# Two attention layers over sixteen batches: weighted sums taken for two groups of heads in one visit, and the transposed maxima moved to the bank of the scores

## The chip, the cores and the metric

The kernel runs on one core of a Trainium2 chip. The metric is the device time of one launch in microseconds (us), the median of several executions. Besides it there is one profiled execution, from which every row below is taken.

## What is computed

Two cross-attention layers follow each other for each of 16 batches. Queries come from `x` (112 rows of 320), keys and values from a context of 375 rows of 192. Cut to what matters:

```python
def _mha(q, k, v, heads):                      # layer 0: 8 heads of 40; layer 1: 20 heads of 16
    scores = jnp.einsum('bhqd,bhkd->bhqk', qh, kh) * d ** -0.5
    probs = jax.nn.softmax(scores, axis=-1)
    return jnp.einsum('bhqk,bhkd->bhqd', probs, vh)
# layer 0
enc, ca = ctx[:, :371], ctx[:, 371:]           # 371 keys, and 4 token rows
hs  = _mha(x @ Wq, enc @ Wk, enc @ Wv)
ca1 = _mha(Q, x, x)        # Q from (ca, Wq_ca): an attention over the 112 rows of x
ca2 = _mha(ca1 @ Wq, ca @ Wk_ca, ca @ Wv_ca)
x1  = (hs + ca2) @ Wout + b_out + x
# layer 1
out = _mha(x1 @ Wq1, ctx @ Wk1, ctx @ Wv1) @ Wo + bo + x1
```

## The kernel before

All engines' programs are written out by hand, in one common order. An iteration t handles parts of several batches, so that independent work stands side by side. It has seven **slots** (0 to 6), and each slot scores one **group** of four heads: in slots 0 and 1 the two groups of layer 0 of batch t, in slots 2 to 6 the five groups of layer 1 of batch t-1. `NUMBER` counts the groups in that order.

A group goes through four steps. `scores` (two heads at a time, "pair 0" and "pair 1", into the two banks of `bankS`) lets VectorE take the negated row maxima (`maximum`, line 773, one reduction per pair). One slot later `transpose_m` (L1172) turns the 112x4 maxima into 4x112, VectorE copies them to `mT` (`copy_mT`, L779), and a DMA of ScalarE's queue (`place_m`) puts them as a row into the queries. Two slots after scoring (`LAG`, the `late` group), `shifted_scores` makes the transposed scores with the maximum subtracted in `bankST` (L1187 layer 0, L1193 layer 1), ScalarE takes the exponentials (`exps`, L573, L574, L577) into one of two halves of `PT` (in `arena`), and `attend` (L1225) makes the weighted sums in `bankO`, whose copy to SBUF is `copy_o` (L790). `attend` issues 12 `matmul` calls per group (24 instructions on the chip, as the operands are fp32), each on only 64 (layer 0) or 32 (layer 1) columns of the array; calls on different columns run at the same time. One `attend` with what surrounds it is called a visit here.

Between these steps, in four **phases** of each slot, stand the **units**: projections and the rest, which take turns in two PSUM banks `bankX0` and `bankX1`. A unit can begin only when the unit two places ahead of it in the list has been drained from its bank (`bank_drained`). The units that matter here, by slot (phases 2 and 3 come after pair 1 of the scores, and `attend` stands between phases 2 and 3):

```python
    ([("V1_0", -1)], [("q1T_0", -1)], [("V1_1", -1)], [("W2", 1), ("PV2", 0)]),                  # slot 0
    ...
    ([("K1_1", 0)], [("S3", 0), ("S2_0", 1)], [("N1b", -2)], [("S2_1", 1)]),                     # slot 2
    ([("K1_2", 0)], [("K0_0", 1)], [("hn1T", -2)], [("K0_1", 1)]),                               # slot 3
    ([("K0_2", 1)], [("p3T", 0), ("N0", 0)], [("out1", -2)], [("q0T_0", 1)]),                    # slot 4
    ([("hn0T", 0), ("V0_0", 1)], [("q0T_1", 1)], [("out0", 0)], [("T2_0", 1)]),                  # slot 5
    ([("x1T", 0), ("V0_1", 1)], [("T2_1", 1)], [("q1", 0)], [("V0_2", 1)]),                      # slot 6
```

S2_0 and S2_1 (L1111) are the scores of the attention over `x`: VectorE takes their maxima (L837), and ScalarE drains each with four exponentials (L595, each with a short read of its sum). K0, K1, V0, V1, q0, q1, out0 and out1 are projections (all L1005). q0T_0, q0T_1 (L1071) and the q1T units (L1078) are transposes of queries; ScalarE drains q0T (L658), and ScalarE and VectorE drain q1T (L666, L829). ScalarE and VectorE drain q1 (L653, L765). N0, N1a and N1b (L1095) transpose the finished sums, hn0T, hn1T and x1T (L1087) the normalised ones. W2 is L1105.

`transpose_m` writes the first 112 columns of `bankO`, which layer 0's weighted sums use as well, so before the change it waits until the last visit's sums are copied (`o_copied`), and `attend` waits until the transposed maxima are copied (`mT_copied`).

Of the kernel before, what the change touches and what calls it, by code (L numbers as in the profile page):

```python
# [85 lines left out]
NUMBER = {g: n for n, g in enumerate(GROUPS)}  # L86

# [24 lines left out]
def xattn_kernel(nc, xT, xpad, ctxT, caS, caT, w_all, w_ca, wqT, bd96, consts, bias, out):  # L112
    g_rows = nc.dram_tensor("g_rows", [B, 3, 32, HID], F32, kind="Internal").ap()

    with ExitStack() as ctx:
# [101 lines left out]
        bank_mT = bankO[0:GROUP, 0:SQ]  # L217
# [334 lines left out]
        def _(act):  # L552
# [10 lines left out]
            def exps(g):  # L563
# [35 lines left out]
            def unit(name, b):  # L599
# [27 lines left out]
                elif kind == "V0":  # L627
                    if i == 0 and b == 0:
                        act.wait_ge(zeroed, 3)
                    elif i == 0:  # L630
                        act.wait_ge(pv_done, NUMBER[0, b - 1, 1] + 1)
# [3 lines left out]
                elif kind == "V1":  # L635
                    if i == 0 and b < 2:
                        act.wait_ge(zeroed, 6 + b)
                    elif i == 0:
                        act.wait_ge(pv_done, NUMBER[1, b - 2, G1 - 1] + 1)
# [91 lines left out]
        def _(dve):  # L731
# [49 lines left out]
            def copy_o(g):  # L781
                layer, b, k = g
                n = NUMBER[g]
                dve.wait_ge(pv_done, n + 1)
                if layer == 0:
                    dst, src = o0T[:, 2 * k:2 * k + 2, :].rearrange("p c q -> p (c q)"), bankO[:, 0:2 * SQ]
                else:
                    at = (2 + n % 2) * SQ
                    dst, src = o1T[:, k, :], bankO[:, at:at + SQ]
# [120 lines left out]
            for t in ITERATIONS:  # L910
                for i in range(SLOTS):
                    g, before, late = scored_at(t, i), scored_at(t, i, 1), scored_at(t, i, LAG)
# [16 lines left out]
                    if late:  # L929
                        copy_o(late)  # L930
# [15 lines left out]
        def _(pe):  # L946
# [61 lines left out]
            def unit(name, b):  # L1008
# [80 lines left out]
                elif kind in ("N0", "N1a", "N1b"):  # L1089
                    layer, k = {"N0": (0, 1), "N1a": (1, 3), "N1b": (1, 4)}[kind]  # L1090
                    pe.wait_ge(o_copied, NUMBER[layer, b, k] + 1)
# [45 lines left out]
            def scores(g, pair):  # L1137
# [25 lines left out]
            def transpose_m(g, attended):  # L1163
                n = NUMBER[g]
                pe.wait_ge(max_done, 2 * n + 2)
                if n > 0:
                    pe.wait_ge(mT_copied, n)
                else:
                    pe.wait_ge(g_split, 4)
                if attended > 0:  # L1170
                    pe.wait_ge(o_copied, attended)
# [27 lines left out]
            def attend(g, transposed):  # L1199
                layer, b, k = g  # L1200
                n = NUMBER[g]
                pe.wait_ge(exp_done, n + 1)
                pe.wait_ge(mT_copied, transposed)
                if n > 0:
                    pe.wait_ge(o_copied, n)
                if k == 0:
                    for i in range(NKC):
                        pe.wait_ge(bank_drained[bank(f"V{layer}_{i}", b)], drained(f"V{layer}_{i}", b))
                src = PT[:, n % 2]
                if layer == 0:  # L1210
                    at_once = [(c, j) for pair in range(2) for c in range(NKC) for j in (2 * pair, 2 * pair + 1)]
                else:
                    at_once = [(c, j) for c in range(NKC) for j in range(GROUP)]
                for c, j in at_once:
                    h = GROUP * k + j
                    if layer == 0:
                        keys = KC if c < 2 else KC - NTOK
                        dst = bankO[64 * (j % 2):64 * (j % 2) + 64, (j // 2) * SQ:(j // 2 + 1) * SQ]
                        v = v0[0:keys, c, 64 * h:64 * h + 64]
                    else:  # L1220
                        keys = KC
                        at = (2 + n % 2) * SQ
                        dst = bankO[32 * j:32 * j + 32, at:at + SQ]
                        v = v1[b % 2][0:keys, c, 32 * h:32 * h + 32]
                    last = nc.tensor.matmul(dst, v, src[0:keys, c, SQ * j:SQ * j + SQ], start=(c == 0),  # L1225
# [118 lines left out]
```

## Time and profile before

| | |
|---|---|
| time, 3 runs | 755.02, 755.55, 756.1 us; median 755.55 |
| profiled execution | 753.38 us, span of its core 751.5 us |
| TensorE matmul / weight load busy | 703.0 us (94%) / 610.3 us (81%) |
| VectorE / ScalarE / GpSimd busy | 472.3 / 404.0 / 295.5 us |
| mean granted TensorE clock | 0.983 of full speed |

The span reaches from the first to the last instruction of the core. PE is TensorE's matmul, PEld its weight load, which normally runs ahead of the matmul before it ends; a busy PE is no proof of a PE at its peak. A row of the timeline gives the start in us from the start of the span, the duration, engine, line, operation, output and inputs, shapes and count, and in brackets the idle time of the engine just ahead of it with what ended it. Idle time matters only on the chain that sets the end.

### The profile page before, as it was taken

The numbers are of one execution on the slowest core, as the hardware profiler recorded it, in microseconds if no ns is written. First come the engines' busy times: TensorE is split into PE (matmuls) and PEld (weight loads), VectorE is DVE, ScalarE is ACT, GpSimd is POOL, SyncE is SP. The second block draws the span as 40 slices with busy tenths as digits, with TensorE's granted clock in tenths as the row PEclk, the third lists the DMA queues.
The fourth block names the chain that finished last, engine by engine and source line by source line (L and its number), as shares of the span: only waits on it lengthen the run. The fifth ranks groups of instructions, "written<-read, shape, count | busy, mean of one in ns | idle before, by whom it ended". The sixth has DMA issues, their size and how long they took to land.

```text
span 751.5 us, 18194 instructions
## 1 busy us (share of the span) xinstructions
PE 703.0 (94%) x6924; PEld 610.3 (81%) x6924; DVE 472.3 (63%) x1028; ACT 404.0 (54%) x923; POOL 295.5 (39%) x401
## 2 busy tenths in 40 slices
PE   8787999999999999999999999999999999999975
PEld 5586888888888888888888888888888888888763
DVE  2653666657576665757576575756667575766662
ACT  2454555555565555565555555556555555654432
POOL 5485662444334253433325344323524542330300
PEclk9889999999999999999999999999999999999996
DMA  9533553443516244252524434261533425051400
GB/s 325 175 96 96 112 133 75 107 80 79 133 47 143 62 119 95 67 118 54 137 60 125 92 80 103 62 142 45 136 81 94 89 76 129 20 137 28 87 7 11
DMA packets 52387, 72.45 MB, mean 96 GB/s; under 512 B 12128, under 2 KB 44256, under 8 KB 52304
## 3 DMA queue, kind: packets, MB, share of 16 engines
q1 hardware_dynamic: 44832, 60.34, 31.7%
q0 software_dynamic: 6144, 9.25, 6.5%
q10 hardware_dynamic: 1328, 1.71, 0.6%
q8 instruction: 57, 0.93, 0.5%
q14 instruction: 26, 0.21, 0.1%
HBM read 20.60 MB, written 4.26 MB: 33 GB/s over the span
## 4 chain that ended last, share of the span: by engine, by line
PE 69%; ACT 13%; DVE 8%; issue 3%; POOL 1%; DMA 1%; SPq 1%; ACTq 0%; POOLq 0%
PE bankX L1005 28%; PE bankO L1225 8%; PE bankST L1193 7%; ACT arena L577 7%; PE bankS L1159 6%; PE bankST L1187 5%; ACT arena L595 3%; DVE negmax L773 2%; DVE q1T L829 2%; PE bankX L1118 2%; PE bankX L1125 2%; PE bankX L1087 2%; PE bankS L1156 2%; ACT q1T L666 2%; PE bankX L1071 2%
## 5 line engine op out<-in xcount | busy, mean ns | idle before, releaser
L773 DVE TENSOR_REDUCE negmax<-bankS 112x2 f32<-112x750 f32 (+1 forms) x224 | 208.7, 932 | 57.0 <-PE bankS L1159 32.7
L494 POOL DMA_DIRECT2D k_stack<-stage x192 | 96.6, 511 | 181.5 <-DVE stage L809 153.9
L577 ACT ACTIVATE arena<-bankST 125x1344 f32<-125x1344 f32 x80 | 103.5, 1294 | 30.9 <-PE bankST L1193 30.9
L1225 PE MATMUL bankO<-arena,v 125*32 125x112 f32 (+2 forms) x2688 | 107.2, 264 | 6.2 <-ACT arena L577 4.4
L1225 PEld LDWEIGHTS bankO<-arena,v 125*32 125x32 f32 (+2 forms) x2688 | 81.2, 117 | 29.0 <-issue 12.7
L1159 PE MATMUL bankS<-k_stack,q1T 112*112 112x376 f32 x320 | 87.8, 355 | 4.1 <-DVE negmax L773 3.0
L1005 PE MATMUL bankX<-ctx_hi,WH 128*120 128x376 f32 (+2 forms) x192 | 69.0, 360 | 3.0 <-DVE qn L765 2.2
L457 POOL TENSOR_TENSOR w2bd<-w2s,cst 96x896 fp32r<-96x896 f32 x16 | 29.9, 1870 | 98.4 <-DVE w2s L765 98.4
L1005 PE MATMUL bankX<-WH,ctx_hi 128*125 128x320 f32 x192 | 66.1, 344 | 0.1
L1193 PE MATMUL bankST<-q1T,k_stack 112*125 112x224 f32 x480 | 65.4, 272 | 0.0
L1005 PE MATMUL bankX<-ctx_hi,WL 128*120 128x376 f32 (+2 forms) x192 | 64.0, 334 | 0.0
L1193 PEld LDWEIGHTS bankST<-q1T,k_stack 112*125 112x125 f32 x480 | 62.0, 188 | 0.8 <-DMA q1T<-mT 0.4
L1005 PE MATMUL bankX<-WL,ctx_hi 128*125 128x320 f32 x192 | 58.5, 312 | 0.0
L1159 PEld LDWEIGHTS bankS<-k_stack,q1T 112*112 112x112 f32 x320 | 49.4, 177 | 8.8 <-DVE negmax L773 6.5
L829 DVE TENSOR_SCALAR q1T<-bankX,odd_rows 128x448 fp32r<-128x448 f32 (+1 forms) x48 | 29.1, 606 | 41.7 <-ACT q1T L666 41.2
L595 ACT ACTIVATE arena<-bankX,negmax 112x112 f32<-112x112 f32 x128 | 43.6, 354 | 21.7 <-DVE negmax L837 21.6
L1005 PE MATMUL bankX<-WH,act_hi 128*112 128x320 f32 x144 | 46.7, 325 | 3.3 <-DVE act_hi L866 1.4
L483 POOL TENSOR_TENSOR xb<-xp,bias_sb 112x320 f32<-112x320 f32 x16 | 13.9, 867 | 88.7 <-DVE x L860 88.6
L779 DVE CAST mT<-bankO 4x112 fp32r<-4x112 f32 x112 | 29.0, 259 | 30.0 <-PE bankO L1172 30.0
L1187 PEld LDWEIGHTS bankST<-q0T,k_stack 121*125 121x125 f32 (+1 forms) x384 | 46.0, 187 | 0.0
L619 ACT ACTIVATE stage<-bankX 128x376 fp32r<-128x376 f32 (+1 forms) x48 | 23.1, 482 | 41.7 <-PE bankX L1005 41.0
L1187 PE MATMUL bankST<-q0T,k_stack 121*125 121x112 f32 (+1 forms) x384 | 44.9, 266 | 0.0
(141 smaller groups left out, 1545.8 us busy)
## 6 DMA issues: line engine op xcount, KB each, us to landing
k_stack<-stage SPq DMA_DIRECT2D x96, 176.2 KB
k_stack<-stage SPq DMA_DIRECT2D x192, 70.5 KB, 2.6
k_stack<-stage POOLq DMA_DIRECT2D x192, 47.0 KB, 2.0
ctx_raw<-in_ctxT SPq DMA_DIRECT2D x16, 376.0 KB, 3.3
k_stack<-stage SPq DMA_DIRECT2D x48, 117.5 KB
xp<-in_xpad SPq DMA_DIRECT2D x16, 224.0 KB, 3.3
x_raw<-in_xT SPq DMA_DIRECT2D x16, 168.0 KB, 2.4
out<-x1b SPq DMA_DIRECT2D x16, 140.0 KB, 3.2
```

What stands on the lines that cost most here:

```text
L457: nc.gpsimd.tensor_tensor(w2bd[:, :, :], w2s[:, :].bitcast(F32).unsqueeze(1).broadcast_to((96, H0, SQ)), mask96.unsqueeze(2).broadcast_to( ...
L494: pool.dma_start(dst, src).then_inc(k1_stacked_pool[b % 2], 16)
L577: nc.scalar.activation(dst[0:KC], bankST[0:KC, :, 0:GROUP * SQ], ACT.Exp).then_inc(exp_done, 1)
L595: last = nc.scalar.activation(prob2[0:SQ, h, :], X[0:SQ, (h % 4) * SQ:(h % 4 + 1) * SQ], ACT.Exp, bias=negmax2[:, h:h + 1], accum_out=sum2 ...
L773: nc.vector.tensor_reduce(negmax[:, n % 2, 2 * pair:2 * pair + 2], bankS[0:SQ, :, 0:keys], axis=AX, op=ALU.max, negate=True).then_inc(max_ ...
L779: nc.vector.tensor_copy(mT[:, n % MT_BUFS, :], bank_mT).then_inc(mT_copied, 1)
L829: nc.vector.tensor_scalar(q1T[:, 4 * i:4 * i + g, 1, :], X[:, 0:g * SQ].rearrange("p (h q) -> p h q", h=g), odd_rows[:, :], None, ALU.mult ...
L1005: last = nc.tensor.matmul(dst, lhs, rhs, start=(n == 0), stop=(n == len(passes) - 1))
L1159: last = nc.tensor.matmul(bankS[0:SQ, j, 0:SKP], q1T[0:ROWS1, h // 2, h % 2, :], k1_stack[b % 2][0:ROWS1, h // 2, :], start=True, stop=True)
L1187: last = nc.tensor.matmul(bankST[0:keys, c, SQ * j:SQ * j + SQ], k0_stack[0:M_ROW0 + 1, h, KC * c:KC * c + keys], q0T[0:M_ROW0 + 1, h, :], ...
L1193: last = nc.tensor.matmul(bankST[0:KC, c, 2 * SQ * pair:2 * SQ * pair + 2 * SQ], k1_stack[b % 2][0:ROWS1, 2 * k + pair, KC * c:KC * c + KC ...
L1225: last = nc.tensor.matmul(dst, v, src[0:keys, c, SQ * j:SQ * j + SQ], start=(c == 0), stop=(c == NKC - 1))
```

## The change

`EPISODES` groups the groups: the two of layer 0 together, and of layer 1 the first two, the next two and the last alone. `attended_at` gives an episode only at the slot in which its last group is late. So `attend` and `copy_o` run four times per batch, in slots 3, 5, 0 and 1, in place of seven times. `shifted_scores` and `exps` keep their places. The sums of two groups stand side by side in `bankO` and are copied by one instruction.

The transposed maxima go to columns 384 to 495 of the second bank of `bankS`, behind the scores of the pair's second head. `transpose_m` now waits for the maxima of pair 0 of the group being scored (they are read from that bank), no longer for `o_copied`. The second matmul of each `scores` call waits for `mT_copied`.

```diff
+EPISODES = [e for b in range(B + 1) for e in
+            ([[(0, b, 0), (0, b, 1)]] if b < B else []) +
+            ([[(1, b - 1, 0), (1, b - 1, 1)], [(1, b - 1, 2), (1, b - 1, 3)], [(1, b - 1, 4)]] if b > 0 else [])]
+EPISODE = {g: n for n, e in enumerate(EPISODES) for g in e}
+def attended_at(t, i):
+    late = scored_at(t, i, LAG)
+    return EPISODES[EPISODE[late]] if late and EPISODES[EPISODE[late]][-1] == late else None
...
-        bank_mT = bankO[0:GROUP, 0:SQ]
+        bank_mT = bankS[0:GROUP, 1, SKP + 8:SKP + 8 + SQ]
...
-                    act.wait_ge(pv_done, n - 1)
+                    act.wait_ge(pv_done, EPISODE[GROUPS[n - 2]] + 1)
...
-                    if late:
-                        copy_o(late)
+                    if attended_at(t, i):
+                        copy_o(attended_at(t, i))
...
                 for j in range(2):
                     h = GROUP * k + 2 * pair + j
+                    if j == 1 and transposed > 0:
+                        pe.wait_ge(mT_copied, transposed)
...
-            def transpose_m(g, attended):
+            def transpose_m(g, scoring):
                 n = NUMBER[g]
-                pe.wait_ge(max_done, 2 * n + 2)
+                if scoring:
+                    pe.wait_ge(max_done, 2 * NUMBER[scoring] + 1)
+                else:
+                    pe.wait_ge(max_done, 2 * n + 2)
...
-                if attended > 0:
-                    pe.wait_ge(o_copied, attended)
...
-                    if late:
-                        attend(late, transposed)
-                        attended = NUMBER[late] + 1
+                    if attended_at(t, i):
+                        attend(attended_at(t, i))
```

Lines move by 12 to 16: L1225 is L1241 after the change, L1111 is L1123, L1159 is L1173, L1005 is L1017, L1095 is L1107, L1087 is L1099, L1156 is L1170.

First place, TensorE in the second half of slot 2 of a middle iteration, before the change: S2_0, pair 1 of the scores, N1b, the visit, S2_1, and pair 0 of slot 3.

```order
L1111 MATMUL bankX<-w2bd,ca_st 112x448 [waits w2_expanded,ca_split,bank_drained1]
L1159 MATMUL bankS<-k_stack,q1T 112x376 [waits max_done]
L1159 MATMUL bankS<-k_stack,q1T 112x376
L1095 MATMUL bankX<-cst,o1T 112x128 [waits o_copied,bank_drained0]
L1225 MATMUL bankO<-arena,v 64x112 [waits bank_drained1,bank_drained0,o_copied,mT_copied,exp_done]
L1225 MATMUL bankO<-arena,v 64x112 x11
L1111 MATMUL bankX<-w2bd,ca_st 112x448 [waits bank_drained1]
```

The same place after the change:

```order
L1123 MATMUL bankX<-w2bd,ca_st 112x448 [waits w2_expanded,ca_split,bank_drained1]
L1173 MATMUL bankS<-k_stack,q1T 112x376 [waits max_done]
L1173 MATMUL bankS<-k_stack,q1T 112x376 [waits mT_copied]
L1107 MATMUL bankX<-cst,o1T 112x128 [waits o_copied,bank_drained0]
L1123 MATMUL bankX<-w2bd,ca_st 112x448 [waits bank_drained1]
```

The visit of twelve calls between S2_0 and S2_1 is gone; S2_1 still waits until its bank (`bank_drained1`, that of S2_0) is drained.

Second place, TensorE in slot 3 right behind, before the change: hn1T, the visit for the second group of layer 0, then K0_1.

```order
L1087 MATMUL bankX<-cst,hn 128x112 [waits bank_drained1,bank_drained0]
L1087 MATMUL bankX<-cst,hn 128x112
L1087 MATMUL bankX<-cst,hn 64x112
L1225 MATMUL bankO<-arena,v 64x112 [waits o_copied,mT_copied,exp_done]
L1225 MATMUL bankO<-arena,v 64x112 x11
L1005 MATMUL bankX<-ctx_hi,WH 120x376 [waits bank_drained1]
```

The same place after the change:

```order
L1099 MATMUL bankX<-cst,hn 64x112
L1241 MATMUL bankO<-arena,v 64x112 [waits bank_drained0,bank_drained1,exp_done,o_copied]
L1241 MATMUL bankO<-arena,v 64x112 x11
L1241 MATMUL bankO<-arena,v 64x112 [waits exp_done]
L1241 MATMUL bankO<-arena,v 64x112 x11
L1017 MATMUL bankX<-ctx_hi,WH 120x376 [waits bank_drained1]
```

Here the twelve calls of the first group now stand ahead of those of the second.

Third place, TensorE from the end of q1 in slot 6 to V1_0 in slot 0, before the change:

```order
L1005 MATMUL bankX<-WL,act_hi 112x320
L1225 MATMUL bankO<-arena,v_1 32x112 [waits o_copied,mT_copied,exp_done]
L1225 MATMUL bankO<-arena,v_1 32x112 x11
L1005 MATMUL bankX<-WH,ctx_hi 125x320 [waits bank_drained0]
L1005 MATMUL bankX<-WH,ctx_lo 125x320
L1005 MATMUL bankX<-WL,ctx_hi 125x320
L1005 MATMUL bankX<-WH,ctx_hi 125x320
L1005 MATMUL bankX<-WL,ctx_hi 125x320
L1156 MATMUL bankS<-k_stack,q0T 112x372 [waits bank_drained0,k0_stacked,max_done]
L1156 MATMUL bankS<-k_stack,q0T 112x372
L1005 MATMUL bankX<-WH,ctx_hi 125x320 [waits bank_drained1]
```

The same place after the change:

```order
L1017 MATMUL bankX<-WL,act_hi 112x320
L1017 MATMUL bankX<-WH,ctx_hi 125x320 [waits bank_drained0]
L1017 MATMUL bankX<-WH,ctx_lo 125x320
L1017 MATMUL bankX<-WL,ctx_hi 125x320
L1017 MATMUL bankX<-WH,ctx_hi 125x320
L1017 MATMUL bankX<-WL,ctx_hi 125x320
L1170 MATMUL bankS<-k_stack,q0T 112x372 [waits bank_drained0,k0_stacked,max_done]
L1170 MATMUL bankS<-k_stack,q0T 112x372 [waits mT_copied]
L1017 MATMUL bankX<-WH,ctx_hi 125x320 [waits bank_drained1]
```

V0_2 now follows q1 directly, and V1_0 (the last row) waits for the bank of q1 with one visit less ahead of it.

## Rows read from the trace of the kernel before

**Rows 1.** The page, part 1: busy time, share, instructions of each engine.

```profile
PE 703.0 (94%) x6924; PEld 610.3 (81%) x6924; DVE 472.3 (63%) x1028; ACT 404.0 (54%) x923; POOL 295.5 (39%) x401
```

**Rows 2.** Waits, all engines: us in total, times, longest.

```profile
PEld bankO L1225 <- issue: 12.7, 63, 0.2
...
PE bankX L1095 <- DVE stage L814: 7.4, 15, 0.5
...
PEld bankX L1111 <- ACT arena L595: 7.0, 13, 0.5
```

**Rows 3.** Timeline, second half of slot 2 of the iteration from 299 us.

```profile
301.86 0.44 PE L1111 MATMUL bankX<-w2bd,ca_st 96*112 96x448 f32 x1
...
302.40 0.61 DVE L837 TENSOR_REDUCE negmax<-bankX 112x4 f32<-112x448 f32 x1
...
302.54 0.13 PEld L1095 LDWEIGHTS bankX<-cst,o1T 128*112 128x112 f32 x1 [0.22 <-DVE p L846]
...
302.82 1.19 PEld L1225 LDWEIGHTS bankO<-arena,v 125*64 125x64 f32 x24 [0.15 <-issue]
...
303.05 0.35 ACT L595 ACTIVATE arena<-bankX,negmax 112x112 f32<-112x112 f32 x1 [0.30 <-DVE negmax L837]
...
304.29 0.21 ACT L595 ACTIVATION_READ_ACCUMULATOR arena<-bankX,negmax 112x1 f32 x1
304.55 0.17 PEld L1111 LDWEIGHTS bankX<-w2bd,ca_st 96*112 96x112 f32 x1 [0.54 <-ACT arena L595]
```

**Rows 4.** Timeline, S2_0 one iteration later.

```profile
345.17 0.44 PE L1111 MATMUL bankX<-w2bd,ca_st 96*112 96x448 f32 x1
```

**Rows 5.** Timeline, the visit in slot 3 and what follows.

```profile
308.98 1.16 PEld L1225 LDWEIGHTS bankO<-arena,v 125*64 125x64 f32 x24 [0.17 <-ACT arena L574]
...
310.29 0.18 PEld L1005 LDWEIGHTS bankX<-ctx_hi,WH 128*120 128x120 f32 x1
```

**Rows 6.** Timeline, end of slot 4 and beginning of slot 5.

```profile
316.17 0.31 PE L1005 MATMUL bankX<-WL,act_hi 128*112 128x320 f32 x1
316.40 0.54 PEld L1225 LDWEIGHTS bankO<-arena,v 125*32 125x32 f32 x24 [0.20 <-issue]
...
317.12 0.60 PE L1071 MATMUL bankX<-cst,qn 112*120 112x112 f32 x4
...
317.75 0.55 ACT L658 ACTIVATE q0T<-bankX 120x448 fp32r<-120x448 f32 x1 [2.76 <-PE bankX L1071]
...
318.35 0.18 PEld L1005 LDWEIGHTS bankX<-WH,ctx_hi 128*125 128x125 f32 x1 [0.24 <-ACT q0T L658]
```

**Rows 7.** Timeline, end of slot 6 to V1_0 in slot 0.

```profile
327.68 0.70 ACT L653 ACTIVATE qn<-bankX 112x640 fp32r<-112x640 f32 x1 [0.27 <-PE bankX L1005]
...
328.42 0.49 DVE L765 SCALAR_TENSOR_TENSOR qn<-bankX,qn 112x320 fp32r<-112x320 f32 x1 [0.97 <-ACT qn L653]
...
329.30 0.18 PEld L1005 LDWEIGHTS bankX<-WH,ctx_hi 128*125 128x125 f32 x1
```

**Rows 8.** Timeline, slot 0: drain of q1T_0, and W2 behind the visit.

```profile
332.80 0.68 DVE L829 TENSOR_SCALAR q1T<-bankX,odd_rows 128x448 fp32r<-128x448 f32 x1 [1.39 <-ACT q1T L666]
...
333.54 0.63 PEld L1105 LDWEIGHTS bankX<-x_raw,bd 128*96 128x96 f32 x6 [0.49 <-DVE q1T L829]
```

**Rows 9.** Timeline, slot 5: copy of the maxima and pair 1.

```profile
320.14 0.26 DVE L779 CAST mT<-bankO 4x112 fp32r<-4x112 f32 x1 [0.52 <-PE bankO L1172]
...
320.25 0.58 PE L1159 MATMUL bankS<-k_stack,q1T 112*112 112x376 f32 x2
...
320.67 0.31 PE L1005 MATMUL bankX<-WH,act_hi 128*112 128x320 f32 x1
```

**Rows 10.** Timeline, slot 4: maximum of pair 0, transpose, N0.

```profile
312.52 0.93 DVE L773 TENSOR_REDUCE negmax<-bankS 112x2 f32<-112x750 f32 x1
...
313.10 0.26 PE L1172 MATMUL bankO<-cst,negmax 112*4 112x112 f32 x1
...
313.96 0.40 PEld L1095 LDWEIGHTS bankX<-cst,o0T 128*112 128x112 f32 x4 [0.73 <-DVE stage L814]
```

More of the change, by code:

```diff
@@ L911, in _ @@
                 for i in range(SLOTS):
-                    g, before, late = scored_at(t, i), scored_at(t, i, 1), scored_at(t, i, LAG)
+                    g, before = scored_at(t, i), scored_at(t, i, 1)
                     if g:
@@ L1090, in unit @@
                     layer, k = {"N0": (0, 1), "N1a": (1, 3), "N1b": (1, 4)}[kind]
-                    pe.wait_ge(o_copied, NUMBER[layer, b, k] + 1)
+                    pe.wait_ge(o_copied, EPISODE[layer, b, k] + 1)
                     cols = [o0T[:, c, :] for c in range(4)] if layer == 0 else [
@@ L1135, in unit, with scores @@
                 last.then_inc(unit_filled, 1)
-            def scores(g, pair):
+            def scores(g, pair, transposed):
                 layer, b, k = g
@@ L1197, in shifted_scores, with attend @@
                 last.then_inc(st_done, 1)
[L1199 to L1203, printed above, removed]
+            def attend(groups):
+                n = EPISODE[groups[0]]
                 if n > 0:
                     pe.wait_ge(o_copied, n)
[L1206 to L1211, printed above, removed]
-                else:
-                    at_once = [(c, j) for c in range(NKC) for j in range(GROUP)]
-                for c, j in at_once:
-                    h = GROUP * k + j
+                else:
+                    pe.wait_ge(g_split, 4)
+                for g in groups:
+                    layer, b, k = g
+                    pe.wait_ge(exp_done, NUMBER[g] + 1)
+                    if k == 0:
+                        for i in range(NKC):
+                            pe.wait_ge(bank_drained[bank(f"V{layer}_{i}", b)], drained(f"V{layer}_{i}", b))
+                    src = PT[:, NUMBER[g] % 2]
@@ L1225, in attend @@
-                    last = nc.tensor.matmul(dst, v, src[0:keys, c, SQ * j:SQ * j + SQ], start=(c == 0),
-                                            stop=(c == NKC - 1))
+                        at_once = [(c, j) for pair in range(2) for c in range(NKC) for j in (2 * pair, 2 * pair + 1)]
+                    else:
+                        at_once = [(c, j) for c in range(NKC) for j in range(GROUP)]
+                    for c, j in at_once:
+                        h = GROUP * k + j
+                        if layer == 0:
+                            keys = KC if c < 2 else KC - NTOK
+                            at = (2 * k + j // 2) * SQ
+                            dst = bankO[64 * (j % 2):64 * (j % 2) + 64, at:at + SQ]
+                            v = v0[0:keys, c, 64 * h:64 * h + 64]
+                        else:
+                            keys = KC
+                            at = (2 + k % 2) * SQ
+                            dst = bankO[32 * j:32 * j + 32, at:at + SQ]
+                            v = v1[b % 2][0:keys, c, 32 * h:32 * h + 32]
+                        last = nc.tensor.matmul(dst, v, src[0:keys, c, SQ * j:SQ * j + SQ], start=(c == 0),
+                                                stop=(c == NKC - 1))
@@ L1249, in _ @@
                     if g:
-                        scores(g, 0)
+                        scores(g, 0, transposed)
                     for u in units_of(t, i, 0):
@@ L1255, in _ @@
                     if before:
-                        transpose_m(before, attended)
+                        transpose_m(before, g)
                         transposed = NUMBER[before] + 1
@@ L1260, in _ @@
                     if g:
-                        scores(g, 1)
+                        scores(g, 1, transposed)
                     for u in units_of(t, i, 2):
                         unit(*u)
-                    if late:
-                        attend(late, transposed)
-                        attended = NUMBER[late] + 1
+                    if attended_at(t, i):
+                        attend(attended_at(t, i))
                     for u in units_of(t, i, 3):
```

28 lines of the change are left out of this document (9 added, 19 removed).

## Prediction

> **What bounds the kernel now.** I read the page's busy times first. TensorE's matmuls are busy for 94% of the span, VectorE 63%, ScalarE 54% [rows 1]. So TensorE's queue sets the end, except where it stands still. The list of waits then says where: in 15 iterations N0 waits 0.5 us each for the drain of K0_2, and 13 times the weight load of S2_1 stands 0.54 us for ScalarE's exponentials. A third entry is of another kind: 63 times the weight loads stop 0.2 us ahead of a visit for nothing that the profile shows [rows 2]. Last I read the timeline of one middle iteration. From one S2_0 to the next it is 43.31 us [rows 3, 4]; this period, paid about 15 times, is what the change has to move. The question at each of the three visits that vanish is: is the next thing on TensorE free to start at once, or does it wait for an engine that doesn't get faster?
>
> **What a visit costs.** In slot 4 the last matmul of out1 starts at 316.17. Matmuls of this kind follow each other at about 0.15 us, so the next unit could start at 316.32; behind the visit it starts at 317.12 [rows 6]. A visit of layer 1 thus costs 0.80 us, of which 0.54 us are its 24 weight loads. A second group in the same visit costs that 0.54 only, if all 48 run at the same pitch. The rest, 0.26 us, is entering and leaving. In layer 0 the 24 loads take 1.16 to 1.19 us, with 0.15 us of stop ahead and 0.15 us behind (308.98 + 1.16 = 310.14, next load 310.29) [rows 3, 5].
>
> The Trainium skill (TensorEngine Tiling (Array Packing), Key Properties) says that changing the tiling mode drains TensorE. The stops of 0.15 to 0.20 us ahead of each visit agree with it. By that rule alone three visits fewer are a plain gain; what it would give stands below as a rival, worked out from rows.
>
> **Slots 2 and 3 (layer 0).** The visit in slot 2 goes, and its 24 instructions come back in slot 3. In slot 2 the visit stands between N1b and S2_1. S2_1 needs S2_0's bank. S2_0 starts at 301.86, VectorE takes its maxima from 302.40 to 303.01, ScalarE's four exponentials run from 303.05 to 304.50, and S2_1's load starts at 304.55 [rows 3]. Nothing in this chain waits for the visit. So S2_1 starts at 304.55 whether the visit is there or not: the visit, 1.19 us of loads and the stop ahead of it, was free, and its removal gives 0. Instead TensorE's load stream stands from 302.67 (end of N1b's load) to 304.55, 1.88 us in place of 0.54. In slot 3 the same 24 instructions cover nothing: what follows, K0_1, starts at 310.29, 0.15 us after the last load [rows 5], so all 1.16 us show. The wait of N0 in slot 4 doesn't absorb them, since its chain (K0_1 and K0_2 on TensorE, their drains on ScalarE and VectorE) begins after the visit. Term A: **+1.16 us**. Bounds: +0.8 if the visit's own stops vanish as well (two of 0.15), +1.4 if the second group costs what a whole visit does.
>
> **Slots 4 and 5.** Behind out1, q0T_0 can start at 316.32 in place of 317.12. ScalarE drains it (its start, 317.75, is set by q0T_0's end, and it had been idle 2.76 us), and that drain sets V0_0 at 318.35 [rows 6]. All of it moves by 0.80. The pair in slot 5 costs 0.54 more. Term B: **-0.26 us**. Bounds: -0.38 (both stops saved: 0.20 ahead and 0.18 between the visit's last load, 316.94, and 317.12) and 0.
>
> **Slots 6 and 0.** Behind q1, V0_2 and pair 0 move up by 0.80. But V1_0 needs the bank of q1: ScalarE copies it from 327.68 to 328.38, VectorE from 328.42 to 328.91 [rows 7], and neither waits for the visit. V1_0 started at 329.30 and can't start before 328.95. So about 0.35 to 0.45 us is gained (its second load comes sooner after a stop), not 0.80; I take 0.40. In slot 0 the pair costs 0.54 more, but W2 behind it stands 0.49 us now, until VectorE has drained q1T_0 at 333.48 [rows 8]. Of that 0.17 us would stay as the stop behind the visit; 0.32 us is absorbed. The pair costs 0.22. Term C: **-0.18 us**. Bounds: -0.37 and +0.14 (nothing absorbed).
>
> **The maxima behind the scores.** New: the second matmul of pair 1 waits for the copy of the maxima. In slot 5 that copy ends at 320.40, the first matmul of the pair starts at 320.25, and the pair's second would start 0.17 us before out0's first at 320.67, so at 320.50, its load some 0.15 us ahead [rows 9]. With about 0.05 us from one engine to the other (as 304.50 to 304.55 above) the load starts 0.05 us late or so. Slots 6 and 0 look the same; in slot 3 it is on the edge; in slots 2 and 4 the copy is early; in slot 1 it is 0.1 us later, but there K1_0 stands for VectorE anyway. Term D: **+0.15 us**. Bounds: 0, and 7 slots x 0.15 = +1.0. Queued behind the waiting matmul is all of TensorE, which is why it counts at all; VectorE's next maximum is late by the same amount.
>
> New as well: `transpose_m` waits for pair 0's maximum. In slot 4 that maximum ends at 313.45 and the transpose started at 313.10, so it is 0.4 us late. Behind it wait p3T and N0, and N0 stands until 313.96 anyway [rows 10]. In the other slots the maximum ends before the transpose starts. Cost 0; without N0's wait it would be 0.4 us. The waits that go (`o_copied` ahead of the transpose, `mT_copied` ahead of the visit) end no stop in the list of waits, so they give nothing. VectorE's three copies fewer are off the path.
>
> **Sum.** 1.16 - 0.26 - 0.18 + 0.15 = +0.87 us per iteration. The stop of S2_1 is there in 13 iterations; the first and last ones have other neighbours, and I count 14 in all: +12.2 us. The profiled execution took 753.38 us (span 751.5, 1.9 around it): 765.6. The median of the runs is 755.55, 2.2 us or 0.3% above the profiled one, so I forecast **767.8, say 768 us**. Bounds added up: lowest 0.8 - 0.37 - 0.37 + 0 = +0.06 per iteration, 757; highest 1.4 + 0 + 0.14 + 1.0 = +2.5, 791. All at one end together is unlikely.
>
> **Rivals.**
> - *The fewer visits pay in full.* Each merged visit saves its two stops, 0.37 us, and nothing becomes late: 3 x 0.37 x 15 = 16.7 us, so 739 us. It decides if S2_1 can start earlier once the visit is gone, that is if ScalarE's exponentials in 303.05 to 304.50 come earlier. Against it: they follow VectorE's maximum, which follows S2_0 and two short operations, not the visit [rows 3]. For it: the other two places do gain. The skill's rule on the drain, named above, would have this outcome. A half form (S2_1's exponentials come 1 us earlier, since some other order results) gives about 753. Together 0.09.
> - *The wait for the copied maxima is the main cost.* The copy stands behind other work of VectorE (drains of K units in slots 2 to 4) and a late one stops TensorE in the middle of pair 1. If each of seven slots loses 0.15 us or more and a restart is paid each time, D is +1.0 or more and the time is 780 or more. It decides where the copy ends over 0.15 us after pair 1 begins; in slot 5 it ends exactly 0.15 after [rows 9]. 0.10.
> - *Covers cancel.* The 1.16 us in slot 3 pushes back work whose inputs then no longer wait (N0's 0.5 us [rows 2], the stops of slot 1), and with B and C the sum is 0: 755.5. Against it: N0's chain begins behind the visit. 0.03.
> - The forecast, slot 2 gives nothing and slot 3 pays: 0.78.
>
> **How the numbers follow.** A change of 0.2%, 1.5 us, is about what a measurement of this kernel can tell. Slower: 0.78 + 0.10, and 0.01 of the half form: 0.89. Within 0.2%: 0.03. Faster: 0.08. The likeliest case alone spans 761 to 776 (terms A and D near their bounds, 0.4 to 1.4 us per iteration times 14 to 15). Below it lies some 0.12, above it 0.10; I reach a little into both: 759 to 778.
>
> **What the changed profile would show.** If right: the period near 44.2 us; at S2_1 (L1123) an idle of about 1.9 us of PEld, released by ScalarE's exponentials, 13 times, some 24 us in the list of waits; one visit of 48 instructions in 2.3 us in slot 3; V1_0 now waits for VectorE's drain of q1; W2 waits for nothing; second scores matmuls wait for L779's copy by under 0.1 us. It is wrong if S2_1 starts less than 2.6 us after S2_0, if the 48 instructions take clearly more or less than twice 1.16 us, if the wait for the copy is long in many slots, or if the granted clock of the middle stretch is lower than now.

## The result, and the profile after

The changed kernel takes 796.82 us (median of 4, 794.62 to 799.32) where the kernel before takes 755.83: ratio 1.0536, 95% interval 1.0502 to 1.057. I had forecast 768 us, 759 to 778. The direction was right and the size was not: 12 us were expected and 41 came.

The page of the changed kernel, span, busy times and the row of granted clock (40 slices, tenths of full speed):

```profile
span 796.8 us, 18066 instructions
...
PE 732.1 (92%) x6924; PEld 639.4 (80%) x6924; DVE 466.4 (59%) x980; ACT 405.5 (51%) x923; POOL 295.1 (37%) x401
...
PEclk9779899999999999798999999798999999799987
```

TensorE runs as many instructions as before [rows 1], yet is busy 29 us longer: the same matmuls take longer in some stretches. The clock row says where. Three stretches make that a sum: the head, up to S2_0 of the third iteration; the middle, twelve iterations; and the tail, the rest. The changed kernel (each row: the stretch and its length in us, busy time and count of PE, PEld, DVE, ACT and POOL, granted clock, share of DMA, GB/s):

```profile
0.00:137.70 137.70, 119.97 (x877) 99.77 (x878) 67.03 (x129) 63.33 (x150) 73.32 (x85) 0.89 0.48 138
137.70:684.80 547.10, 518.77 (x5127) 460.82 (x5126) 337.62 (x720) 296.79 (x685) 205.49 (x288) 0.97 0.37 88
684.80:796.80 112.00, 93.37 (x925) 78.82 (x924) 61.80 (x131) 45.41 (x90) 16.32 (x28) 0.89 0.22 47
```

The same three of the kernel before:

```profile
0.00:128.60 128.60, 112.38 (x877) 92.99 (x878) 67.98 (x133) 63.18 (x150) 73.39 (x85) 0.95 0.52 148
128.60:648.40 519.80, 503.61 (x5126) 444.84 (x5126) 342.13 (x756) 295.79 (x685) 205.79 (x288) 1.00 0.39 93
648.40:751.50 103.10, 87.01 (x925) 72.46 (x924) 62.15 (x139) 45.05 (x90) 16.36 (x28) 0.95 0.24 51
```

So the profiled execution lost 9.1 us in the head, 27.3 in the middle and 8.9 in the tail. Single iterations of the changed kernel, from S2_0 to S2_0:

```profile
271.93:316.16 44.23, 41.86 (x429) 37.12 (x429) 28.09 (x60) 24.64 (x58) 17.10 (x24) 1.00 0.39 92
316.16:364.57 48.41, 46.05 (x429) 41.07 (x429) 28.17 (x60) 24.91 (x58) 17.12 (x24) 0.89 0.36 84
364.57:411.96 47.39, 45.03 (x429) 40.09 (x429) 28.18 (x60) 24.79 (x58) 17.12 (x24) 0.93 0.36 85
```

At full clock an iteration takes 44.23 us against 43.3 before [rows 3, 4]; that is the sum of the prediction, which said 44.2. But in some iterations the clock is granted at 0.89 or 0.93, and they take 3 to 4 us more. Of the twelve of the middle, seven take 44.2 to 44.3 us, one 45.7, two 47.4 and two 48.4. Twelve times 0.92 us are 11 of the 27 us of the middle; the other 16 are the clock.

Now the places of the prediction, in the undisturbed iteration. Slot 2, S2_0 to S2_1, which answers to [rows 3]:

```profile
271.93 0.44 PE L1123 MATMUL bankX<-w2bd,ca_st 96*112 96x448 f32 x1
...
272.60 0.13 PEld L1107 LDWEIGHTS bankX<-cst,o1T 128*112 128x112 f32 x1 [0.21 <-DVE p L858]
...
274.35 0.21 ACT L608 ACTIVATION_READ_ACCUMULATOR arena<-bankX,negmax 112x1 f32 x1
...
274.62 0.17 PEld L1123 LDWEIGHTS bankX<-w2bd,ca_st 96*112 96x112 f32 x1 [1.89 <-ACT arena L608]
274.62 0.46 PE L1123 MATMUL bankX<-w2bd,ca_st 96*112 96x448 f32 x1 [1.70 <-ACT arena L608]
```

S2_1 starts 2.69 us after S2_0, as before the change (301.86 to 304.55 [rows 3]): the visit was free and its removal gave nothing. Slots 3 to 0, which answer to [rows 5 to 8]:

```profile
279.05 2.32 PEld L1241 LDWEIGHTS bankO<-arena,v 125*64 125x64 f32 x48 [0.17 <-issue]
...
281.51 0.18 PEld L1017 LDWEIGHTS bankX<-ctx_hi,WH 128*120 128x120 f32 x1
...
292.52 1.12 PEld L1241 LDWEIGHTS bankO<-arena,v 125*32 125x32 f32 x48 [0.20 <-issue]
...
299.50 0.49 DVE L778 SCALAR_TENSOR_TENSOR qn<-bankX,qn 112x320 fp32r<-112x320 f32 x1 [0.97 <-ACT qn L666]
...
300.05 0.18 PEld L1017 LDWEIGHTS bankX<-WH,ctx_hi 128*125 128x125 f32 x1 [0.53 <-DVE qn L778]
...
303.24 1.12 PEld L1241 LDWEIGHTS bankO<-arena,v 125*32 125x32 f32 x48 [0.19 <-issue]
...
304.52 0.63 PEld L1117 LDWEIGHTS bankX<-x_raw,bd 128*96 128x96 f32 x6 [0.17 <-issue]
```

The 48 loads take exactly twice the 1.16 us of 24, and 1.12 against twice 0.54 in layer 1; there is one stop ahead and one behind. V1_0 now waits 0.53 us for VectorE's drain of q1, and W2 no longer waits for an engine. All of this was forecast.

What wasn't: the same place one iteration later, where the matmuls behind the stop take 0.52 us in place of 0.33.

```profile
318.85 0.71 PE L1123 MATMUL bankX<-w2bd,ca_st 96*112 96x448 f32 x1 [1.69 <-ACT arena L608]
...
319.99 0.52 PE L1017 MATMUL bankX<-ctx_hi,WH 128*128 128x376 f32 x1
...
320.30 0.52 PE L1017 MATMUL bankX<-ctx_lo,WH 128*128 128x376 f32 x1
```

```profile
275.43 0.33 PE L1017 MATMUL bankX<-ctx_lo,WH 128*128 128x376 f32 x1
```

They start 0.31 us apart (319.99 to 320.30) where they start 0.17 apart at full clock: TensorE has gone from 2.4 to 1.2 GHz. Stretches around the stop of S2_1 in the changed kernel:

```profile
300.00:316.85 16.85, 16.77 (x188) 14.93 (x188) 10.11 (x22) 8.77 (x16) 5.10 (x4) 1.00 0.36 85
...
316.85:318.85 2.00, 0.31 (x2) 0.12 (x1) 1.62 (x4) 1.65 (x10) 0.00 (x0) 0.72 0.00 1
318.85:329.00 10.15, 10.15 (x63) 9.63 (x65) 4.72 (x11) 4.41 (x15) 4.79 (x10) 0.55 0.21 38
```

TensorE had been busy without a gap to speak of for 16.85 us at full clock, its matmuls then stood for 1.69 us, and it worked without any gap for 10 us at nearly half speed. A mean of 0.72 over the 2.00 us of the stretch with the stop, between 1.00 and 0.50, means 1.1 us at the lower level: the clock fell inside the stop. It needn't: one iteration on, the stop is as long, but the matmuls behind it still run at full pace, and only the twelve of the shifted scores take 2.41 us in place of 1.40. There the fall came about 1.7 us after TensorE had gone back to work.

```profile
367.26 0.46 PE L1123 MATMUL bankX<-w2bd,ca_st 96*112 96x448 f32 x1 [1.69 <-ACT arena L608]
...
368.59 0.33 PE L1017 MATMUL bankX<-ctx_hi,WL 128*128 128x376 f32 x1
368.76 2.41 PE L1200 MATMUL bankST<-q0T,k_stack 121*125 121x112 f32 x12
```

The stop of S2_1 is there 13 times, 12 times at the start of a period of the middle and once more at 684.8. The clock falls in or just behind six of them.

### The profile page after: what moved, and what is told of

The parts are those of the page before. It is cut to its first block, busy times and chain, and to the rows that moved or that the text cites. A ratio compares the mean times of both kernels' runs of the same rounds, so it can differ in the third digit from the quotient of the medians.

```text
span 796.8 us, 18066 instructions
## 1 busy us (share of the span) xinstructions
PE 732.1 (92%) x6924; PEld 639.4 (80%) x6924; DVE 466.4 (59%) x980; ACT 405.5 (51%) x923; POOL 295.1 (37%) x401
## 4 chain that ended last, share of the span: by engine, by line
PE 78%; ACT 7%; DVE 5%; issue 2%; POOL 1%; DMA 1%; SPq 1%; ACTq 0%; POOLq 0%
PE bankX L1017 30%; PE bankO L1241 12%; PE bankS L1173 7%; PE bankST L1206 6%; PE bankST L1200 6%; ACT arena L590 3%; ACT arena L608 3%; PE bankS L1170 3%; PE bankX L1090 2%; PE bankX L1099 2%; PE bankX L1130 2%; PE bankX L1137 2%; PE bankX L1145 1%; PE bankX L1083 1%; ACT qn L666 1%
## 5 line engine op out<-in xcount | busy, mean ns | idle before, releaser
L1241 PE MATMUL bankO<-arena,v 125*32 125x112 f32 (+2 forms) x2688 | 103.4, 270 | 2.8 <-ACT arena L590 2.8
L1241 PEld LDWEIGHTS bankO<-arena,v 125*32 125x32 f32 (+2 forms) x2688 | 87.9, 123 | 17.1 <-issue 16.7
L1173 PE MATMUL bankS<-k_stack,q1T 112*112 112x376 f32 x320 | 95.7, 378 | 6.0 <-DVE negmax L786 3.9
L1017 PE MATMUL bankX<-ctx_hi,WH 128*120 128x376 f32 (+2 forms) x192 | 73.8, 385 | 2.4 <-ACT arena L608 1.7
L1017 PE MATMUL bankX<-WH,ctx_hi 128*125 128x320 f32 x192 | 66.2, 345 | 3.0 <-DVE qn L778 2.9
L1017 PE MATMUL bankX<-ctx_hi,WL 128*120 128x376 f32 (+2 forms) x192 | 68.8, 358 | 0.0
L1173 PEld LDWEIGHTS bankS<-k_stack,q1T 112*112 112x112 f32 x320 | 55.3, 187 | 13.6 <-DVE negmax L786 6.5
L1017 PE MATMUL bankX<-WL,ctx_hi 128*125 128x320 f32 x192 | 58.1, 310 | 0.0
L638 ACT ACTIVATE stage<-bankX 120x376 fp32r<-120x376 f32 (+1 forms) x48 | 23.2, 484 | 65.7 <-PE bankX L1017 64.8
L792 DVE CAST mT<-bankS 4x112 fp32r<-4x112 f32 x112 | 29.1, 260 | 46.1 <-PE bankS L1185 46.0
L1200 PEld LDWEIGHTS bankST<-q0T,k_stack 121*125 121x125 f32 (+1 forms) x384 | 54.7, 218 | 0.0
L1200 PE MATMUL bankST<-q0T,k_stack 121*125 121x112 f32 (+1 forms) x384 | 53.0, 295 | 0.0
L826 DVE TENSOR_TENSOR stage<-bankX,stage 120x376 fp32r<-120x376 f32 (+1 forms) x48 | 26.2, 545 | 42.1 <-ACT stage L638 42.1
L1017 PE MATMUL bankX<-WH,act_hi 128*112 128x320 f32 x144 | 46.7, 325 | 3.0 <-DVE act_hi L878 1.4
```

What stands on the lines that cost most here:

```text
L792: nc.vector.tensor_copy(mT[:, n % MT_BUFS, :], bank_mT).then_inc(mT_copied, 1)
L1017: last = nc.tensor.matmul(dst, lhs, rhs, start=(n == 0), stop=(n == len(passes) - 1))
L1173: last = nc.tensor.matmul(bankS[0:SQ, j, 0:SKP], q1T[0:ROWS1, h // 2, h % 2, :], k1_stack[b % 2][0:ROWS1, h // 2, :], start=True, stop=True)
L1200: last = nc.tensor.matmul(bankST[0:keys, c, SQ * j:SQ * j + SQ], k0_stack[0:M_ROW0 + 1, h, KC * c:KC * c + keys], q0T[0:M_ROW0 + 1, h, :], ...
```

## The experiments

"Period" is the mean time from S2_0 to S2_0 over twelve iterations of the profiled execution, from the third to the fifteenth; before it is 519.8 / 12 = 43.32 us.

**The bank of the maxima alone.** `EPISODES` with seven single groups; the slices of `copy_o` follow, here and in all runs with single groups.

```diff
-            ([[(0, b, 0), (0, b, 1)]] if b < B else []) +
-            ([[(1, b - 1, 0), (1, b - 1, 1)], [(1, b - 1, 2), (1, b - 1, 3)], [(1, b - 1, 4)]] if b > 0 else [])]
+            ([[(0, b, 0)], [(0, b, 1)]] if b < B else []) +
+            ([[(1, b - 1, k)] for k in range(G1)] if b > 0 else [])]
```

> Seven visits as before, only the transposed maxima in the bank of the scores. Theory (two costs: the stop of S2_1 that the missing visit uncovers, and a TensorE clock that falls in it): neither is here, so the period is 43.31 us + 0.15 for the waits on the copied maxima, 755.8 + 2 = 758 us, granted clock 0.98. Rival (the bank move is what costs: transposes and pair 1 wait, TensorE is less busy and its clock falls): period 44.5 us or more, clock under 0.96, over 775 us.

762.1 us (median of 6), ratio 1.008 [1.0047, 1.0114]. The period is 521.74 / 12 = 43.48 us, +0.16: term D as forecast, 1.9 us in the middle, at full clock. The total missed by 4 us, and the rest of the 7 us lies at the ends. The profiled execution is the slowest of the six, 766.15 us. Its head takes 133.5 us at a clock of 0.91, 4.9 us more than before; but two kernels below whose heads are the same instruction for instruction (pairs again, and filled tail) took 129.1 and 134.2 us, so that much comes and goes between executions. Its tail takes 109.0 us at 0.90, 5.9 us more than before. In that tail stand all seven of these waits, of the second scores matmul for the copied maxima, which the kernel before hasn't:

```profile
PEld bankS L1174 <- DVE mT L792: 3.6, 7, 0.7
```

So in the last iteration the moved bank costs more than in the middle.

**Pairs in layer 1, single groups in layer 0.** Only the first line of the edit above.

> Layer 0's two groups visited one by one in slots 2 and 3 as before, layer 1 in pairs as in the change (five visits per batch), bank of the maxima as in the change. Theory: S2_1's stop stays covered, so the clock stays (0.98), and what is left are terms B, C and D of the prediction, -0.26 - 0.18 + 0.15 = -0.29 us per iteration: 755.8 - 4 = 752 us, period 43.0. Rival (pairs of visits as such, in either layer, thin out TensorE's work so that its clock falls): clock under 0.96 and over 775 us.

755.85 us (median of 10), ratio 1.000 [0.9968, 1.0031]. The middle:

```profile
129.10:646.10 517.00, 504.35 (x5126) 444.62 (x5126) 339.19 (x732) 295.59 (x685) 205.30 (x288) 1.00 0.40 93
646.10:755.10 109.00, 92.22 (x925) 77.20 (x924) 62.17 (x133) 45.15 (x90) 16.31 (x28) 0.88 0.23 48
```

Period 43.08, -0.24 (forecast -0.29), at full clock throughout. The forecast total, 752, was missed: in the profiled execution the 2.8 us won in the middle went in the tail, which ran at 0.88 and took 5.9 us more. Pairs as such don't lower the clock of the middle, and the rival falls.

**The pair in layer 0 alone.** Only the second line.

> Only layer 0's two groups in one visit in slot 3, layer 1 one by one. Theory: term A and D, 1.16 + 0.15 = 1.31 us per iteration, where the clock is full: period 44.6 us, and S2_1 stops TensorE 1.9 us in 13 iterations, in which the clock falls in some: clock 0.94 to 0.96, 755.8 + 18 + 20 to 30 = 794 to 804 us. Rival (the clock has other causes than this stop): 774 us at clock 0.98.

816.83 us (median of the three executions that agree; 819.86 with the profiled one, which took 832.11), ratio 1.0823 [1.0757, 1.089]: slower even than the change itself, and than I expected. S2_1 stands 1.9 us 13 times, as in the change, but in the profiled execution every one of the middle iterations takes 47.75 us, none 44.6, and they differ from each other by less than 0.05 us. The mean clock of the other three was higher, 0.920 to 0.934 against 0.909; how many iterations fell in them isn't known. The stop goes with the fall of the clock; that it can take every iteration here and only some in the change was not in the theory.

**The stop filled.** Nine matmuls whose result nobody reads, in `bankO`, which is free then.

```diff
                     for u in units_of(t, i, 2):
                         unit(*u)
+                    if i == 2 and 2 <= t < B - 1:
+                        for _ in range(9):
+                            nc.tensor.matmul(bankO[:, 0:376], WH[:, 0:128], WH[:, 0:376], start=True, stop=True)
                     if attended_at(t, i):
                         attend(attended_at(t, i))
```

> The changed kernel with nine matmuls of 376 columns more (about 0.17 us each, 1.5 us in all, results not used) between N1b and S2_1, in the stop of 1.7 to 1.9 us. Theory: TensorE does work there and the clock no longer falls: clock 0.98, period 44.2 us throughout, 768 us, as the prediction's sum without a clock had it. Rival (the clock falls for another reason than the stop, or the added work itself costs): 797 us or more, clock 0.95 or less.

780.15 us (median of 4), ratio 1.0328. Timeline of its slot 2 (L1282 is the fill):

```profile
313.83 1.80 PE L1282 MATMUL bankO<-WH 128*128 128x376 f32 x9
...
315.76 0.17 PEld L1123 LDWEIGHTS bankX<-w2bd,ca_st 96*112 96x112 f32 x1 [0.45 <-ACT arena L608]
```

and its middle stretch:

```profile
136.14:666.90 530.76, 521.18 (x5234) 462.66 (x5234) 337.27 (x720) 295.55 (x685) 205.23 (x288) 1.00 0.39 91
```

Full clock in every middle iteration, period 44.23 us. More work made the kernel 17 us faster, 16 of them in the middle. The theory said 768; the 12 us more lie at the two ends, where nothing was filled (136.1 and 115.3 us in the profiled execution, against 128.6 and 103.1 before).

**The same work behind S2_1.** The nine matmuls after phase 3 of slot 2, so that the stop stays.

> The changed kernel with the same nine matmuls (1.5 us, results not used) behind S2_1, so that TensorE has as much work more but the stop ahead of S2_1 stays. Theory (the stop is what lets the clock fall): the clock still falls in the middle iterations, as in the changed kernel or in another rhythm; with the added 1.5 us per iteration 805 to 830 us, clock 0.95 or less. Rival (TensorE's total share of busy time per iteration decides): the share is as high as with the filled stop, so all middle iterations are at full clock with a period of 44.24 + 1.5 = 45.8 us, about 800 us, clock 0.97.

816.09 us (median of 3), ratio 1.0769. Its middle stretch and its wait:

```profile
137.60:702.40 564.80, 536.54 (x5235) 479.96 (x5234) 339.44 (x720) 295.78 (x685) 205.26 (x288) 0.97 0.36 85
```

```profile
PEld bankX L1123 <- ACT arena L608: 24.5, 13, 1.9
```

Two of the twelve iterations take the 45.8 us of full clock, the other ten 47.2 to 47.4. Same work as in the filled stop, other place, and the clock falls: the stop counts, not the total of work.

**Less fill.** Four matmuls in place of nine.

> The changed kernel with four matmuls (0.7 us) in the stop ahead of S2_1 in place of nine. Theory (how long TensorE stands there decides): a stop of 1.0 us is left, more than the 0.5 of before and less than 1.9; the clock falls in fewer middle iterations than in the changed kernel or in none: between 780 and 795 us. Rival (any such stop is enough, or the nine worked by chance): 795 us or more, clock 0.945.

786.72 us (median of 3), ratio 1.0397. The list of waits and the middle stretch:

```profile
PE bankX L1123 <- ACT arena L608: 13.0, 13, 1.0
```

```profile
138.90:669.90 531.00, 510.94 (x5176) 452.33 (x5174) 337.32 (x720) 295.61 (x685) 205.33 (x288) 1.00 0.38 91
```

With 1.0 us of stop left the clock doesn't fall in the middle at all. The medians of the two fills are 6.6 us apart, the profiled executions 2.6, all of it at the ends (784.9 - 531.0 = 253.9 us outside the middle, against 782.2 - 530.8 = 251.4); the rest is the spread of the executions, 778.9 to 784.1 us with nine matmuls and 784.1 to 788.9 with four.

**One pair only.** Layer 1's first two groups as a pair, all others single.

> Maxima in the bank of the scores, layer 0 one by one, of layer 1 only the first two groups in a pair (term B with D, no C). Theory: period 43.46 (bank alone) - 0.26 = 43.20 us; the pair of the third and fourth group (term C) is then worth 43.20 - 43.08 = 0.12 to 0.18 us. Rival (the gain is all in one of the two pairs): period 43.46 or 43.08.

763.01 us (one run). Period 518.11 / 12 = 43.18 us: the pair of slots 4 and 5 is worth 0.30 us (term B, forecast 0.26), and that of slots 6 and 0, from 43.18 to 43.08, 0.10 us (term C, forecast 0.18).

**Ends without the stop.** The filled kernel, with layer 0's groups one by one in batches 0, 1 and 15.

```diff
-            ([[(0, b, 0), (0, b, 1)]] if b < B else []) +
+            ([[(0, b, 0), (0, b, 1)]] if 2 <= b < B - 1 else [[(0, b, 0)], [(0, b, 1)]] if b < B else []) +
```

> The changed kernel with the stop filled as before (nine matmuls), and layer 0's two groups one by one in the batches 0, 1 and 15, where the fill isn't. Theory: with the clock kept in the first and last iterations too, what is left is the prediction's sum without a clock: S2_0 of the third iteration at 129 to 131 us as in the kernel before (137 in the changed one), period 44.24, total 767 to 770 us, clock 0.975 or more. Rival (the 8 us more at each end are waits and not the clock): 778 us or more.

772.01 us (median of 4), ratio 1.02 [1.0158, 1.0242].

```profile
0.00:129.50 129.50, 113.36 (x877) 93.38 (x878) 67.16 (x131) 63.13 (x150) 73.36 (x85) 0.95 0.50 147
129.50:660.40 530.90, 521.20 (x5235) 462.57 (x5234) 337.24 (x720) 295.84 (x685) 205.72 (x288) 1.00 0.38 91
660.40:770.10 109.70, 92.83 (x934) 77.92 (x933) 62.00 (x132) 45.20 (x90) 16.34 (x28) 0.90 0.23 48
```

The head takes 129.5 us at 0.95, against 137.7 at 0.89 in the changed kernel and 128.6 before: most of the 9 us of the head were the clock too. Not all: with single groups in batches 0 and 1 this kernel doesn't pay term A there either, which by 1.16 us each is up to 2.3 us. The middle is as forecast. The tail still takes 6.6 us more than before, at 0.90, of which its first iteration pays term A, 1.16 us; it also has the seven waits for the copied maxima. The few us above the 767 to 770 of the theory are there.

**Work left out of the kernel before.** The visit in slot 2 does 2 of its 12 calls; most of the weighted sums of layer 0's first group are not computed.

```diff
                     at_once = [(c, j) for pair in range(2) for c in range(NKC) for j in (2 * pair, 2 * pair + 1)]
+                    if k == 0:
+                        at_once = [(0, 0), (0, 1)]
...
-                                            stop=(c == NKC - 1))
+                                            stop=(c == NKC - 1 or (layer == 0 and k == 0)))
```

> The kernel before, with 10 of the 12 calls of the visit in slot 2 left out (the weighted sums of layer 0's first group are not computed, output not the reference's), and nothing done elsewhere for it. Theory: the visit was free, so S2_1 still starts 2.69 us after S2_0 and an iteration with full clock takes 43.3 us as before; but TensorE now stands some 1.5 us there, and the clock falls in some iterations: less work and yet 775 to 800 us. Rival 1 (the visit was not free): period 42.2 us, 740 us. Rival 2 (free, and the stop alone doesn't lower the clock): 755 us.

812.11 us (median of 4), ratio 1.0714 [1.0665, 1.0763]. Timeline of a slot 2, and the stretch of twelve iterations:

```profile
321.75 0.44 PE L1111 MATMUL bankX<-w2bd,ca_st 96*112 96x448 f32 x1
...
324.43 0.26 PEld L1111 LDWEIGHTS bankX<-w2bd,ca_st 96*112 96x112 f32 x1 [1.50 <-ACT arena L595]
324.44 0.72 PE L1111 MATMUL bankX<-w2bd,ca_st 96*112 96x448 f32 x1 [1.29 <-ACT arena L595]
...
325.58 0.52 PE L1005 MATMUL bankX<-ctx_hi,WH 128*128 128x376 f32 x1
```

```profile
130.60:704.00 573.40, 545.51 (x4886) 484.42 (x4885) 341.88 (x756) 298.80 (x685) 205.75 (x288) 0.89 0.36 84
```

S2_1 still starts 2.69 us after S2_0, so the visit was free, and rival 1 falls. Nothing was added anywhere, 240 instructions are gone from the middle (x5126 to x4886), and the kernel is 57 us slower, since the clock falls in every iteration, each 47.8 us. It was more than I had expected (775 to 800). Emptying that stop does it alone, with no merged visit and no moved bank.

**Pairs in layer 1 with the maxima in their old bank.** The kernel before with pairs of layer 1 only; `bank_mT`, the waits of `transpose_m` and `attend` as before.

> Kernel before with pairs of visits in layer 1 only, and the transposed maxima in their old bank with their old waits. Theory: terms B and C without D. Measured so far: bank alone +0.15 us per iteration, bank and layer-1 pairs -0.23, so pairs alone -0.38 us: period 42.93, and -5.5 us against before if head and tail keep their clock: 749 to 751 us. Rival (the old waits of the transpose for the copied sums take the gain back, as the sums of a pair are copied later): 754 us or more, period 43.3.

752.11 us (median of 12) beside 756.59 of before, ratio 0.993 [0.990, 0.996]: faster. Its three stretches:

```profile
0.00:129.80 129.80, 112.96 (x877) 93.45 (x877) 67.39 (x131) 63.02 (x150) 73.67 (x85) 0.95 0.51 147
129.80:644.50 514.70, 499.66 (x5128) 445.03 (x5126) 339.19 (x732) 295.52 (x685) 205.35 (x288) 1.00 0.40 94
644.50:746.60 102.10, 85.50 (x925) 72.79 (x924) 61.47 (x133) 44.99 (x90) 16.31 (x28) 0.96 0.24 51
```

Period 42.89 us (forecast 42.93), 0.43 less than before. In the old bank the pairs keep their whole gain. Beside the same pairs with the bank moved (ratio 1.000) that is some 5 us less, of which 2.3 are in the middle (517.0 - 514.7) and the rest at the ends.

**The same again, beside a filled tail.**

> The kernel with pairs in layer 1 and the maxima in their old bank once more, beside its version with the filled tail and beside the kernel before. Theory: 5 us less than the kernel before again, period 42.9 us, ratio 0.993. Rival (the first result was luck of where the clock falls at the ends): ratio within 0.998 to 1.002.

> The kernel with pairs in layer 1 and the maxima in their old bank, with three or four unused matmuls of 376 columns in the waits of the last iteration (behind pair 1's scores and, at the very end, behind the shifted scores). Theory: the clock falls some 15 us ahead of the end in that kernel, in waits of 0.9 to 1.4 us; filling them keeps it full until nearly the end: 2 to 4 us less than the same kernel without them (746 to 749 against 750 to 752 us). Rival (the waits there are on VectorE and ScalarE, so TensorE's clock doesn't matter, or the fill delays): no difference within 1 us, or slower.

The edit of the second (the same wait and three matmuls also stand behind pair 1's scores where `t == B`):

```diff
                     if late:
                         shifted_scores(late)
+                    if late and (t > B or (t == B and i >= 5)):
+                        pe.wait_ge(mT_copied, transposed)
+                        pe.wait_ge(o_copied, attended)
+                        for _ in range(4):
+                            nc.tensor.matmul(bankO[:, 0:376], WH[:, 0:128], WH[:, 0:376], start=True, stop=True)
```

Again: 750.85 us (median of 12) beside 755.24, ratio 0.9942 [0.9914, 0.997], period 514.96 / 12 = 42.91 us. Filled tail: 749.95 us (median of 9), ratio 0.9928 [0.9903, 0.9953]. The first result holds. The filled tail was to give 2 to 4 us and the medians differ by 0.9, so that expectation failed: its tail keeps the clock at 0.99 and takes 102.54 us, but that of the unfilled kernel took 102.1 us at 0.96 in one profiled execution and 105.9 at 0.89 in the other, and the two intervals overlap for the most part.

## Why the prediction was wrong

- **What bounds the kernel, and that each vanished visit has to be asked what stands behind it.** Right. It gave 44.2 us for the period, measured 44.24.
- **Term A, slots 2 and 3, +1.16 us.** Right: from 43.08 (pairs in layer 1) to 44.24 us (all pairs, clock kept) is 1.16. S2_1 came 2.68 to 2.70 us after S2_0 in the middle of every kernel of this study.
- **Terms B, -0.26, C, -0.18, and D, +0.15.** Measured -0.30, -0.10 and +0.16 per iteration of the middle. Their sum is right to 0.05 us. Counting D alike in 14 iterations, 2.1 us, was too little: with the bank moved alone the kernel is 6.8 us slower, 1.9 of it in the middle, and the pairs of layer 1 lose some 5 us by it, 2.3 in the middle. In the profiled executions of kernels with layer 0 one by one at the end the tail takes 109.0 to 109.7 us with the new bank and 102.1 to 106.8 with the old. How much of that the seven late copies cost themselves and how much the lower clock of that tail isn't separated.
- **The step that failed** is the price of the stop in term A. The prediction saw that "TensorE's load stream stands from 302.67 (end of N1b's load) to 304.55, 1.88 us in place of 0.54", and wrote "its removal gives 0". A longer stop was taken to cost only its own time. It costs the clock as well: in the middle 16 us of the 27, and in the head most of the 9. The granted clock stood only in the last sentence, as something that would prove me wrong, with no price, no rival and no chance. The rivals I had were about waits. With the clock kept, the middle of the changed kernel takes 530.8 us in place of 547.1, and with the head kept too the total is 772 us, inside the range that I gave; the kernel that shows it doesn't pay term A in three of the batches, up to 3.5 us.
- **The rival of the wait for the copied maxima** (0.10) wasn't the main cost: term D was as small as said in the middle. But it has something in it: I had said under 0.1 us per wait, and in the middle twelve loads of layer 0's scores wait up to 0.2 us, in the tail seven of layer 1's up to 0.7. **The gain in full** (0.09) fell with S2_1, which never came earlier, and so did its half form. What gain there was lies at the visits of layer 1, where nothing waited behind the visit for as long: the version with pairs in layer 1 alone and the old bank is 0.6 to 0.7% faster.
- The lower end of the added bounds, 0.06 us in 14 iterations above 755.55, is 756.4 us and not 757; nothing hangs on it.

The Trainium skill (TensorE: Matmul & The Clock Gate, Why this matters for your kernels) names idle gaps between bursts of matmuls as what brings the clock down, but longer ones than the 1.3 to 1.7 us between matmuls seen here. The measurement decides: in this kernel such gaps, once per iteration in an engine that was busy for 95% of the middle, were enough.

**What stays open:** which of the stops the clock falls at. It does at six of the thirteen in the changed kernel, in ten of twelve iterations with work added behind the stop, and in all with the pair in layer 0 alone (in its profiled execution) or with the visit left out, whose stop is even shorter (1.3 us against 1.7). So the length of the stop doesn't decide alone: 1.7 us was harmless in seven places of the changed kernel, and 1.3 us, in another kernel, never was. The traces say that the moment counts too. In the kernel with the work behind the stop, the granted clock of the 2 us that begin 2.7 us after S2_0 is 0.59, 0.71 and 0.82 in three iterations one after another, so the fall comes later each time, and in the fourth it doesn't come (1.00); then the same begins again. What sets that moment is not shown. Nor was it settled what makes the tail of most variants run at 0.88 to 0.90 in place of 0.95.

## What to carry to other kernels

Before moving work off a saturated engine's path, look whether that work was covering a wait: if what stands behind it waits for a chain that doesn't start with it, taking it away saves nothing and its new place costs all of it. On TensorE price the gap a second time: every gap that the change opens or lengthens beyond those that the kernel already bears is a chance that the clock halves for the next several us (3 to 10 us at a time here), and a row of granted clock by iteration shows it. A cheap test of that suspicion is to put matmuls that nobody needs into the gap: if the kernel gets faster with more work, it was the clock. And a wait that is small in the steady loop can be longer in the last iteration, where less work stands beside it: 0.2 us became 0.7 here.

## What the runs showed of the hardware

- Leaving out 240 of 5126 TensorE instructions in the middle iterations made the kernel 7% slower; it left a stop of 1.3 us between matmuls once per iteration: period 47.8 us against 43.3, granted clock 0.89 against 1.00.
- The clock fell inside a stop of 1.69 us that followed 16.85 us of nearly unbroken work at full clock, and then 10 us of unbroken work ran at 0.55. One iteration later it fell about 1.7 us behind the end of the same stop, with TensorE at work. Matmuls of 376 columns started 0.31 us apart in place of 0.17.
- A visit of column-tiled matmuls costs 0.15 to 0.20 us of stopped weight loads ahead and 0.14 to 0.17 behind, whatever its length (24 or 48 loads); two groups of layer 1 in one visit are worth 0.10 to 0.30 us, by what waits behind them, and the two of layer 0 cost 1.16 us, since the first visit had been free.
